# Gated cross-attention block with a Hadamard feed-forward: chunk 0 by halves of the channels, LayerNorm 2 of chunk 0 applied behind gate and up

## The reference

```python
# per channel, over t:  y_t = (A*p + E*v_t) / (A*q + E), in closed form sums of
# exp(k_s + decay*(t-s)) * v_s over the same without v_s
x = x + tanh(g_xattn[0]) * wkv(w, u, k=layernorm(x), v=ctx)
# feed-forward of h = layernorm(x), 256 -> 1024 -> 256
h = fwht(h * SU_ug) / 64
up, gate = h @ W_up.T * (s_up * 64), h @ W_gate.T * (s_gate * 64)
h = fwht(silu(gate) * up * SU_dp) / 64
x = x + tanh(g_ffn[0]) * (h @ W_down.T * (s_dp * 64))
```

## Time and profile before

| | us |
|---|---|
| median of 3 runs | 118.2 (117.4 to 118.34) |
| span of the profiled execution | 117.3 |
| TensorE busy | 99.5 |
| VectorE busy | 70.0 |
| ScalarE busy | 67.6 |
| POOL busy | 61.3 |

### The profile page before, as it was taken

How to read it: one execution, slowest core, us unless ns; L and a number is a source line. 1 busy time by engine, 2 the same in 40 slices (tenths; PEclk the granted TensorE clock), 3 DMA queues, 4 the chain that set the end, 5 groups by cost and what they waited for, 6 DMA issues and landing times.

```text
span 117.3 us, 1942 instructions
## 1 busy us (share of the span) xinstructions
PE 99.5 (85%) x684; PEld 89.2 (76%) x684; DVE 70.0 (60%) x145; ACT 67.6 (58%) x146; POOL 61.3 (52%) x76
## 2 busy tenths in 40 slices
PE   0056584799969999999999999999999999869980
PEld 0044463664559978789999999999999999769970
DVE  0688289936696798797998456874137531231311
ACT  4589566013689942999562899645459732504400
POOL 7102899689909897953550805732520633222430
PEclk9999999999999999999999999999999999999999
DMA  2799999200000000000000020000020000020002
GB/s 72 171 329 409 334 399 408 101 0 3 0 3 6 0 0 0 0 0 6 0 0 0 3 95 0 0 0 0 6 89 0 3 0 6 0 89 0 3 0 89
DMA packets 3074, 7.69 MB, mean 66 GB/s; under 512 B 468, under 2 KB 854, under 8 KB 2936
## 3 DMA queue, kind: packets, MB, share of 16 engines
q1 hardware_dynamic: 3064, 7.57, 17.9%
HBM read 6.52 MB, written 1.05 MB: 65 GB/s over the span
## 4 chain that ended last, share of the span: by engine, by line
PE 70%; DMA 9%; DVE 8%; ACT 4%; SPq 3%; issue 2%; POOL 1%; POOLq 1%; ACTq 0%; DVEq 0%
PE UG L900 38%; PE OD L938 12%; DMA V<-in_ct 9%; PE KZ L938 6%; PE UG L827 5%; PE FX L859 5%; PE FX L868 2%; DVE X L327 1%; DVE XT L762 1%; PE VB L876 1%; DVE SP_ L640 1%; SPq L389 1%; ACT S L596 1%; DVE OD L705 1%; PE VB L881 1%
## 5 line engine op out<-in xcount | busy, mean ns | idle before, releaser
L461 POOL TENSOR_TENSOR HL<-H,HH 128x256 fp32r<-128x256 f32 x32 | 25.7, 813 | 32.4 <-ACT HH L587 32.4
L776 DVE SCALAR_TENSOR_TENSOR H<-S,ALPHA,UG 128x256 f32<-128x256 f32 x32 | 15.0, 478 | 22.3 <-ACT S L596 22.1
L596 ACT ACTIVATE S<-UG,VT 128x256 f32<-128x256 f32 x32 | 15.1, 472 | 17.5 <-PE UG L900 17.4
L900 PE MATMUL UG<-FH,WTH 128*128 128x256 f32 x128 | 21.4, 289 | 0.8 <-ACT FH L581 0.8
L900 PE MATMUL UG<-FL,WTH 128*128 128x256 f32 x128 | 20.4, 281 | 0.0
L900 PE MATMUL UG<-FH,WTL 128*128 128x256 f32 x128 | 20.3, 280 | 0.0
L900 PEld LDWEIGHTS UG<-FH,WTH 128*128 128x128 f32 x128 | 17.8, 189 | 2.1 <-issue 1.9
L900 PEld LDWEIGHTS UG<-FH,WTL 128*128 128x128 f32 x128 | 17.4, 189 | 0.0
L900 PEld LDWEIGHTS UG<-FL,WTH 128*128 128x128 f32 x128 | 17.4, 188 | 0.0
L587 ACT ACTIVATE HH<-H 128x256 fp32r<-128x256 f32 x32 | 13.2, 412 | 4.5 <-DVE H L776 4.2
L938 PE MATMUL OD<-HH,MH 128*128 128x256 f32 x40 | 11.3, 283 | 1.6 <-DVE XT L762 1.6
(11 more groups left out here) (120 smaller groups left out, 200.5 us busy)
## 6 DMA issues: line engine op xcount, KB each, us to landing
WN<-in_weights SPq DMA_DIRECT2D x4, 512.0 KB, 9.8
DN<-in_w_down SPq DMA_DIRECT2D x1, 1024.0 KB, 8.6
out<-XT SPq DMA_DIRECT2D x3, 256.0 KB, 2.5
V<-in_ct SPq DMA_DIRECT2D x2, 258.0 KB, 10.8
V<-in_ct SPq DMA_DIRECT2D x1, 516.0 KB, 12.5
X<-in_x SPq DMA_DIRECT2D x2, 256.0 KB, 4.2
XT<-in_xt SPq DMA_DIRECT2D x2, 256.0 KB, 10.8
X<-in_x SPq DMA_DIRECT2D x1, 512.0 KB, 11.5
```

Source lines behind the costliest of these rows:

```text
L461: pool.tensor_tensor(HL[:, q % JT, 0:n], ring(H, q), HH[:, q % JT, 0:n].bitcast(F32), ALU.subtract).then_inc(h_lo, 1)
L596: act.activation(ring(S, q), gate_part(q), ACT.Silu, scale=VT[:, V_SGATE + j:V_SGATE + j + 1]).then_inc(silu_ready, 1)
L776: dve.scalar_tensor_tensor(out=ring(H, q), in0=ring(S, q), scalar=ALPHA[:, j:j + 1], in1=up_part(q), op0=ALU.mult, op1=ALU.mult).then_inc( ...
L900: return pe.matmul(dst.rearrange("p (g n) -> p g n", n=GT), w[:, m, j, t, :], f[:, chunks, t, :], start=start, stop=stop, skip_group_check ...
```

## The change

- **Chunk 0 by halves.** Its WKV runs as stages with names ending in 0, each on one half of the channels (256 columns), in two PSUM banks of their own. Its values are multiplied with the gate tanh in `av0`; y goes to `YT`, and the transform is made in parts, x (`x_part`) and each half of y (`y_part`). POOL adds y to x later (`x1_0`).
- **LayerNorm 2 of chunk 0 behind gate and up.** The raw transform is split (`raw_hi`, `raw_lo`) and multiplied in slots 0 to 3; VectorE scales both halves of the bank there (`scale`). From slot `RAW` = 4 on the scaled `F0` is used.
- **LayerNorm 2 elsewhere.** The variance lands with tokens on partitions (`var`: one column), POOL takes the power -1/2 (`rstd2`), TensorE spreads it (`spread`), ScalarE copies the row (`row`).
- **The down product of chunk 0 unsplit:** two f32 products a slot, from `H0` and `DB`; no high and low parts in slots 0 to 7. `m_hi` and `m_lo` serve later chunks.
- **A third level of butterflies** (`fly` 8 to 11) on VectorE, and one product for each `m`.
- All weights arrive turned; `w` is one product with the identity. The centred matrix comes from TensorE whole. The ramp is an iota on POOL. Two small loads go to ScalarE's queue, and SP's order is new. `LAG` is 5.

The tables and the queue:

```diff
+RAW = 4
 
 
 PE_STAGES = {
-    -1: [("keys", 0), ("center", 0), ("w", 0), ("w_rest", 0), ("w", 1), ("w", 2), ("w", 3), ("w_rest", 1), ("w_rest", 2), ("w_rest", 3),
-        ("keys", 1), ("fwht", 0), ("m", 0), ("ones", 0), ("keys", 2), ("m", 1), ("m_rest", 0)],
-    0: [("keys", 3), ("m_rest", 1)],
-    4: [("m", 2), ("fwht", 1)],
-    5: [("m_rest", 2), ("ones", 1), ("m", 3)],
-    7: [("m_rest", 3)],
-    11: [("fwht", 2)],
-    12: [("ones", 2)],
-    19: [("fwht", 3)],
-    21: [("ones", 3)],
+    -1: [("keys0", 0), ("keys0", 1), ("center", 0), ("w", 0), ("w", 1), ("w_rest", 0), ("x_part", 0), ("keys", 1), ("w", 2),
+        ("w_rest", 1), ("y_part", 0), ("w_rest", 2), ("y_part", 1), ("w", 3)],
+    0: [("var", 0), ("w_rest", 3)],
+    1: [("spread", 0), ("m", 0)],
+    2: [("m", 1)],
+    3: [("m", 2), ("keys", 2), ("m", 3)],
+    4: [("fwht", 1)],
+    5: [("var", 1)],
+    6: [("spread", 1)],
+    7: [("keys", 3)],
+    10: [("fwht", 2)],
+    11: [("var", 2)],
+    12: [("spread", 2)],
+    17: [("fwht", 3)],
+    20: [("var", 3)],
+    21: [("spread", 3)],
 }
 ACT_STAGES = {
-    -1: [("setup", 0), ("signs", 0), ("decay", 0), ("keys", 0), ("pads", 0), ("w_hi", 0), ("w_lo", 0), ("recip", 0), ("w_hi", 1),
-        ("w_hi", 2), ("w_lo", 1), ("w_hi", 3), ("w_lo", 2), ("w_lo", 3), ("w_hi", 4), ("square", 0), ("keys", 1), ("rstd2", 0),
-        ("m_hi", 0), ("w_hi", 5), ("f_hi", 0), ("m_lo", 0), ("m_hi", 1), ("keys", 2), ("recip", 1), ("m_lo", 1), ("keys", 3)],
-    0: [("w_hi", 6)],
-    3: [("w_hi", 7), ("square", 1), ("m_hi", 2)],
-    5: [("m_lo", 2), ("exp_block", (("rstd2", 1), ("recip", 2))), ("m_hi", 3), ("f_hi", 1)],
-    6: [("m_lo", 3)],
-    9: [("x_hi", 2)],
-    11: [("square", 2)],
-    12: [("exp_block", (("rstd2", 2), ("recip", 3))), ("f_hi", 2)],
-    17: [("x_hi", 3)],
-    19: [("square", 3)],
-    20: [("exp_block", (("rstd2", 3),))],
+    -1: [("setup", 0), ("signs", 0), ("pads", 0), ("keys0", 0), ("keys0", 1), ("decay", 0), ("center", 0), ("w_hi", 0),
+        ("w_hi", 1), ("recip0", 0), ("w_lo", 0), ("recip0", 1), ("w_hi", 2), ("w_hi", 3), ("keys", 1), ("w_lo", 1),
+        ("raw_hi", 0), ("w_lo", 2), ("w_hi", 4), ("square", 0), ("w_hi", 5), ("w_hi", 6), ("recip", 1), ("w_lo", 3),
+        ("w_hi", 7), ("row", 0), ("m_copy", 0), ("silu", 0), ("m_copy", 1), ("m_hi", 0), ("f0_hi", 0), ("m_hi", 1),
+        ("m_copy", 2), ("m_hi", 2)],
+    0: [("exp_block", (("keys", 2),))],
+    1: [("m_copy", 3)],
+    2: [("square", 1)],
+    4: [("m_hi", 3)],
+    5: [("row", 1)],
+    7: [("f_hi", 1), ("exp_block", (("keys", 3), ("recip", 2))), ("x_hi", 2)],
+    8: [("square", 2)],
+    9: [("exp_block", (("recip", 3),)), ("row", 2)],
+    12: [("f_hi", 2)],
+    13: [("x_hi", 3)],
+    16: [("square", 3)],
+    20: [("row", 3)],
     21: [("f_hi", 3)],
 }
 DVE_STAGES = {
-    -1: [("stats1", 0), ("setup_rows", 0), ("norm1", 0), ("setup_shift", 0), ("stats1", 1), ("center", 0), ("scan_a", 0), ("mix_den", 0),
-        ("av", 0), ("scan_av", 0), ("mix_num", 0), ("norm1", 1), ("estimate", 0), ("newton", 0), ("x1", 0), ("stats1", 2), ("stats1", 3),
-        ("outs", 0), ("scan_a", 1), ("mix_den", 1), ("root", 0), ("f_scaled", 0), ("av", 1), ("f_lo", 0), ("scan_av", 1), ("mix_num", 1),
-        ("estimate", 1), ("newton", 1), ("x1", 1)],
-    3: [("scan_av", 2), ("scan_a", 2), ("mix_den", 2)],
-    5: [("scan_a", 3), ("mix_num", 2), ("root", 1), ("f_scaled", 1), ("estimate", 2), ("f_lo", 1)],
-    6: [("newton", 2), ("x1", 2)],
-    8: [("mix_den", 3), ("scan_av", 3), ("mix_num", 3), ("x_lo", 2)],
-    12: [("root", 2), ("f_scaled", 2), ("f_lo", 2)],
-    15: [("estimate", 3)],
-    16: [("newton", 3), ("x1", 3), ("x_lo", 3)],
-    20: [("root", 3), ("f_scaled", 3)],
-    21: [("f_lo", 3)],
+    -1: [("pads0", 0), ("stats1", 0), ("rows", 0), ("norm1", 0), ("shift", 0), ("stats1", 1), ("scan_a0", 0), ("mix_den0", 0),
+        ("scan_a0", 1), ("av0", 0), ("mix_den0", 1), ("scan_av0", 0), ("av0", 1), ("mix_num0", 0), ("scan_av0", 1),
+        ("estimate0", 0), ("mix_num0", 1), ("estimate0", 1), ("newton0", 0), ("newton0", 1), ("scan_a", 1), ("mix_den", 1),
+        ("av", 1), ("raw_lo", 0), ("scan_av", 1), ("var_eps", 0), ("mix_num", 1), ("fly", 8), ("fly", 9), ("estimate", 1),
+        ("stats1", 2), ("fly", 10), ("f_scaled", 0), ("newton", 1), ("norm1", 2), ("fly", 11)],
+    0: [("outs", 0)],
+    1: [("f0_lo", 0), ("x1", 1)],
+    2: [("stats1", 3)],
+    3: [("scan_a", 2), ("var_eps", 1), ("mix_den", 2)],
+    4: [("norm1", 3), ("f_scaled", 1), ("scan_av", 2), ("f_lo", 1)],
+    5: [("mix_num", 2)],
+    6: [("estimate", 2)],
+    7: [("newton", 2), ("x1", 2), ("x_lo", 2)],
+    8: [("scan_a", 3)],
+    9: [("mix_den", 3), ("var_eps", 2), ("scan_av", 3), ("mix_num", 3), ("estimate", 3), ("f_scaled", 2)],
+    11: [("newton", 3), ("x1", 3)],
+    13: [("f_lo", 2)],
+    15: [("x_lo", 3)],
+    17: [("var_eps", 3)],
+    19: [("f_scaled", 3)],
+    20: [("f_lo", 3)],
 }
 POOL_STAGES = {
-    -1: [("rstd1", 0), ("rstd1", 1), ("fly", 0), ("fly", 1), ("fly", 2), ("error", 0), ("fly", 3), ("fly", 4), ("fly", 5), ("fly", 6),
-        ("rstd1", 2), ("rstd1", 3), ("norm1", 2), ("fly", 7), ("w_lo", 4), ("norm1", 3), ("av", 2), ("error", 1), ("av", 3), ("w_lo", 5)],
-    2: [("w_lo", 6), ("sum", 1), ("w_lo", 7)],
-    4: [("error", 2)],
-    9: [("sum", 2)],
-    11: [("error", 3)],
-    18: [("sum", 3)],
+    -1: [("rstd1", 0), ("fly", 0), ("fly", 1), ("rstd1", 1), ("norm1", 1), ("fly", 2), ("error0", 0), ("error0", 1),
+        ("fly", 3), ("fly", 4), ("fly", 6), ("fly", 5), ("fly", 7), ("rstd2", 0), ("w_lo", 4), ("error", 1), ("rstd1", 2),
+        ("w_lo", 5), ("w_lo", 6), ("m_lo", 0), ("m_lo", 1), ("av", 2), ("w_lo", 7), ("sum", 1), ("rstd1", 3), ("m_lo", 2),
+        ("rstd2", 1), ("x1_0", 0), ("error", 2), ("av", 3), ("sum", 2), ("m_lo", 3)],
+    3: [("rstd2", 2)],
+    8: [("error", 3)],
+    16: [("sum", 3)],
+    17: [("rstd2", 3)],
 }
 
 
@@ -115,20 +137,19 @@
 
 
 
...
+            if n >= 8:
+                wait_shared(eng, "fly", 4, 5, 6, 7)
+                s = [DN[:, 4 * i + 2 * (n % 2):4 * i + 2 * (n % 2) + 2, :].rearrange("p j c -> p (j c)") for i in range(2)]
+                eng.tensor_tensor(m_part(DB, n - 8), *s, ALU.subtract if n >= 10 else ALU.add).then_inc(done, 1)
+                return
...
 
             load_x(0)
-            sp.dma_start(VT[:, :], vecs).then_inc(vec_in, 16)
-            sp.dma_start(VR[:, :], rows).then_inc(row_in, 16)
             sp.dma_start(HI[:, :], consts).then_inc(const_in, 16)
-            sp.dma_start(STEP[:, :, :].rearrange("p t n -> p (t n)"), steps).then_inc(step_in, 16)
             load_x(1)
+            sp.dma_start(DN[:, :, :], w_down).then_inc(down_in, 16)
+            load_ctx(0)
             load_w(0, 0)
-            sp.dma_start(DN[:, :, :], w_down).then_inc(down_in, 16)
+            load_xt(0)
             load_w(1, 0)
-            load_ctx(0)
-            load_xt(0)
+            load_ctx(1)
             load_w(0, 1)
             load_w(1, 1)
+            load_xt(1)
             load_x(2)
-            load_ctx(1)
-            load_xt(1)
             load_ctx(2)
             load_xt(2)
             for g in range(LAST):
@@ -416,17 +474,18 @@
 
         @block.gpsimd
```

The new functions and stages (semaphore bookkeeping cut):

```diff
+                elif name == "m_copy":
+
+                    act.wait_ge(m_full, M_FULL.index(g) + 1)
+                    act.activation(m_part(DB, g), fill(("m", g))[:, :], ACT.Copy).then_inc(m_copied, 1)
...
+                elif name == "raw_hi":
+
+                    act.wait_ge(f_full, 1)
+                    for t in range(CT):
+                        act.activation(FH[:, FIRST, t, :], FX[:, t * GT:(t + 1) * GT], ACT.Copy).then_inc(raw_hi, 1)
...
-                act.wait_ge(filled, FILLED["up" if width(q) == GT else "gate", q])
+                if q < RAW:
+                    act.wait_ge(scaled, q + 1)
+                else:
+                    act.wait_ge(filled, FILLED["up" if width(q) == GT else "gate", q])
                 act.activation(ring(S, q), gate_part(q), ACT.Silu, scale=VT[:, V_SGATE + j:V_SGATE + j + 1]).then_inc(silu_ready, 1)
-                if q:
+                if q > JT:
                     hi(q - 1)
 
             for q in range(-1, SLOTS):
...
+            def first(name, t):
+
+                part = slice(t * GB * PAD, (t + 1) * GB * PAD)
+                steps, decay = EXPS0[t][:, 0:GB * PAD], D[:, t, :, :].rearrange("p b q -> p (b q)")
+                if name == "scan_a0":
+                    dve.wait_ge(padded_set, t + 1)
+                    dve.wait_ge(pads0, CT)
+                    dve.wait_ge(pads, 3)
+                    dve.wait_ge(a0_ready, t + 1)
+                    dve.tensor_tensor_scan(SQ[:, part], decay, steps, 0.0, ALU.mult, ALU.add).then_inc(scanned_a0, 1)
+                elif name == "mix_den0":
...
+                elif name == "av0":
+                    if t == 0:
+                        dve.wait_ge(ctx_in[0], 16)
```

(72 more changed lines are left out.)

598 lines of the change are left out of this document (337 added, 261 removed).

## The result

The changed kernel takes 121.5 us (median of 4 runs, 121.2 to 123.4); the kernel before took 118.1 us beside it. The ratio is 1.026, with a 95% interval of 1.020 to 1.032: slower, where 116.4 us and faster were forecast. The profiled execution took 121.39 us with a span of 119.6 us, against 117.3 us of span before.

The account below looks back on a forecast made before the run. Bound: the start of TensorE's unbroken stretch plus its work in it. Span 117.3 - 1.7 - 0.7 - 0.35 + 1.0 = 115.5 us; the same step from the median 118.2 gives 116.4 us, range 113.0 to 119.8.

Parts of the forecast that it names:

- part 1: Start to raw transform of chunk 0: second weight piece at 13.8 us, clock rise at 19.0, transform full at 23.3.
- rival 4: Start not brought forward: second weight piece at 14.8 us or later, or a queue holds the halves; 117.4 to 118.4; chance 0.18.
- Part 2: Raw transform to up(4): VectorE's list before hidden(0) sets up(4) at 38.8 us against 40.5, -1.7 us.
- part 3: TensorE's work from up(4) on: products and rests gone, others added, -0.7 us in sum.
- part 4: The tail: LAG 5 leaves five pairs of down products, one more first half fills a wait, -0.35 us.
- part 5: New stalls, up(4) to up(14): VectorE's 27.9 us of work against TensorE's 26.9, +1.0 us, ends 0 and +5.0.
- Rival 2: VectorE bounds groups 0 and 1, its SBUF passes stretched beside POOL: 122 us, 120 with two thirds; chance 0.17.
- rival 1: VectorE's SBUF instructions take their lower ends: up(4) at 36.8 us, no stall, 113.5 us; chance 0.23.
- rival 3: TensorE's clock rises late: lower level until the raw transform, full at 28.4 us; time 121.5 us; chance 0.07.
- idle TensorE of over 3 us between 40 and 70 us: Sign that the forecast is wrong and Rival 2 holds.
- VectorE over 95% busy: Sign that the forecast is right: VectorE's busy share from 25 to 60 us.

Follow-up runs that it names:

- e3: Kernel before with its two small loads (vectors and decay row) issued by ScalarE: 117.9 us, ratio 1.000.
- e10: Kernel before with the two output instructions of a finished chunk ahead of the hidden product of their slot: 117.0 us, ratio 0.985.
- e16: Changed kernel with a third setting of the engines' lists for slots 7 to 14, nothing computed otherwise: 119.9 us, ratio 1.022 to the kernel before.
- e5: Changed kernel with the reciprocal of chunk 2 ahead of the keys of chunk 3 on ScalarE: 121.5 us, ratio 1.026 to the kernel before.
- e7: Changed kernel with POOL's four low parts of M and its addition for chunk 0 cut to one column: 118.8 us, ratio 1.011 to the kernel before.
- e15: Changed kernel with only the block of chunk 3 loosened (some VectorE and ScalarE steps moved to slots 10 and 11): 121.5 us, no ratio.
- e12: Changed kernel with LAG 4 instead of 5: 123.8 us, ratio 1.034 to the kernel before.
- e9: Changed kernel, VectorE's block of chunk 3 spread over slots 9 to 12, chunk 2's transform, variance and spread one slot later: 124.9 us, ratio 1.050.
- e13: Changed kernel with a second setting of the engines' lists for slots 7 to 17: 123.7 us, ratio 1.048 to the kernel before.
- e14: e13 with the two output instructions of each chunk ahead of the hidden product of their slot: 122.6 us, ratio 1.038 to the kernel before.

## Why the prediction was wrong

**The start, part 1: right.** The second weight piece was there at 14.6 us (4.37 + 10.26), 0.8 later than forecast and 0.2 short of rival 4's mark of 14.8 (its products began at 13.55 before), TensorE's records are fast from 17.8 us (forecast 19.0), the raw transform is full at 23.0 us (forecast 23.3).

**Part 2, up(4) at 38.8 us: nearly right, and worth less than it seemed.** It came at 39.22 us. The four butterflies took 4.9 us instead of 3.4: two at the lower bound of 0.68, two at 1.76, above the upper bound of 1.27 (least, median and most of the four, in ns):

```profile
L419 DVE TENSOR_TENSOR DB<-DN x4: 682/1222/1766, 27.4 to 35.2; 128x512 f32<-128x512 f32 x4
```

The rule of the Trainium skill quoted there (SBUF — State Buffer, Who interferes with whom) is borne out where the two meet: 1.76 us is the 0.68 of the instruction and 1.08 of the 1.27 to 1.3 that POOL's instruction beside it takes alone. It held for two of the four butterflies only. norm2 took 2.10 us, near the 2.02 of the pair in the earlier trace rows. The list ended only 0.5 us late all the same, since the transform was 0.3 us early and the steps beside butterflies and norm2 took about 0.9 us less than priced. The comparison was off as well, since the profiled execution of before was a late one: e3, which differs up to there in two small loads only, had up(4) at 38.42 us, and e10, with the same code up to there, at 40.84, with the clock at its lower level from 22 to 28 us. Twelve profiles of the kernel after and of kernels like it up to slot 4 have it between 37.4 and 40.3 us, 39.1 on average. Against the mean of the three profiles of before, 39.9, the gain of the start is about 0.8 us rather than 1.7 (an estimate, for the three lie 2.4 us apart).

The ledger of the span, by the landmarks, in us:

| | forecast | measured |
|---|---|---|
| part 2, up(4) | -1.7 | -1.1 |
| part 3, TensorE's work from up(4) on | -0.7 | -0.1 |
| part 4, LAG 5 and the tail | -0.35 | -0.3 |
| part 5, new stops | +1.0 | +3.8 |
| sum | -1.8 | +2.3 |

**Part 3 was mis-sized by 0.6 us.** Without the four waits, up(4) to up(14) would take 31.1 - 3.8 = 27.3 us, where I had 26.9; the kernel before took 28.7, and LAG 5 took a pair of down products (0.71) out, so the work fell by 0.7, not by 1.05. From up(14) to the end of the last up product it takes 41.6 us (70.34 to 111.92) instead of 41.0 (69.04 to 110.01): +0.6, where +0.35 was forecast. The rows of the single groups were right (f32 pair 0.86 us, keys 3, spread 0.45, variance 0.34). What was missing lies between groups, in tenths: 0.2 around the transform of chunk 1 (up(4) to up(5) is 1.42 + 1.73 by rows, and takes 3.36), 0.1 behind the first variance. An up product behind the one-column variance takes 1.51 to 1.53 us instead of 1.42. A change between f32 and split products alone costs nothing: in e16 an unsplit pair and the up product behind it take 2.28 us (53.14 to 55.42), 0.86 + 1.42. What takes these tenths is not shown.

**Part 4 was right.** One pair less ahead of the last up (-0.71), and a tail of 7.7 us (111.9 to 119.6) instead of 7.3 (110.0 to 117.3): -0.3. The wait for POOL's last low parts is shorter there, not gone: the chain of waits still ends through one, at 112.86 us.

**Part 5 failed in its mechanism, and by 2.8 us.** It took VectorE's durations (23.8 to 31.9 us, middle 27.9) against TensorE's 26.9 and called the difference the stall. The amount was right: VectorE was busy for 27.0 us. But VectorE idled too, for 4.1 us in that stretch, so it was not the bound. The stops hang on chains across engines: at 60.19 us reciprocal of chunk 2 (behind keys 3 on ScalarE; e5's swap takes 0.7 us out), error on POOL, Newton, x1, high part; at 48.25 the eps step, late behind a scan of 2.28 us beside POOL (gone in e7), and POOL's power; at 66.68 POOL's power of 1.55 us (in e7 the wait is gone); at 70.34 six steps, four of them of chunk 3, that stand on VectorE ahead of hidden(10) (gone in e15, with the same work on its list). A sum over one engine has no term for a step's place in its queue. e16 shows what the place was worth: the same steps, 2.6 us less in that stretch and 1.6 us less in all.

**From span to time.** Of the error of 5.1 us, 4.1 lie in the span (119.6 against 115.5). The other 1.0 is the step from span to time: I took 0.9, the distance from the profiled span to the median of other runs. It is 1.74 to 1.86 us in every run here, so the profiled execution of before, span 117.3, took about 119.1 us (an estimate from that distance) and was 0.9 us slower than the median it was set against.

**The rivals.** Rival 2 had the right size (120 to 122) and half the mechanism. Stretching beside POOL is real and was worth 2.1 us of span (e7; 2.4 from up(0) on), but the point from which the rival decides, 31 us of VectorE work, was never reached. Rivals 1, 3 and 4 did not come. Of the signs, idle TensorE of over 3 us between 40 and 70 us came by the slots (3.8 us) and not quite by the brackets (2.5 us); VectorE over 95% busy did not come: 17.4 of 21 us from 39 to 60.

**What stays open.** What takes the tenths between TensorE's groups; why the change still costs 2% with its lists set right; why e12's run at full clock took 123.2 us; and why a clock falls in one run and not in the next.

## What to carry to other kernels

Before a step is moved, follow it through the queues: whose wait stands in front of it, and who stands behind it on each engine. A sum of durations on the busiest engine says how much work there is, not when it is there; three settings of the same lists took 124.9, 123.7 and 119.9 us. And look for a small stop first: one pair of instructions ahead of a wait instead of behind it brought 1.5%, as much as the whole change was forecast to bring.

## What the runs showed of the hardware

**A stop of TensorE can cost its clock as well.** The granted clock was 0.50 after the stop of 4.48 us (e9), 0.55 from 68 to 70 us after one of 2.95 us (e13), and in e12, e14 and e15 0.50 in stretches between 36 and 42 us after stops of 1.35 and 0.81 us that the kernel after has too, without a fall in its profile. The Trainium skill (TensorE: Matmul & The Clock Gate, Part 1) says that the clock falls back to its lower level after idle time, and that what a kernel sees of the clock varies from run to run. The rows agree on both. The lower clock stayed for some 3 to 7 us. In e15 it moved up(5) by 1.3 us (4.63 us from up(4), 3.36 in the kernel after), but up(7) by only 0.8 (10.4 against 9.6 us), because TensorE then came too late to stop ahead of the first spread. These are the clocks of 2 us stretches in e12 (columns as in the earlier trace rows):

```profile
34.00:36.00 2.00, 1.19 (x6) 0.52 (x4) 2.00 (x3) 0.26 (x1) 2.00 (x2) 0.92 0.00 0
36.00:38.00 2.00, 1.49 (x4) 0.64 (x4) 2.00 (x6) 1.97 (x4) 0.22 (x1) 0.50 0.00 0
38.00:40.00 2.00, 2.00 (x11) 2.00 (x11) 1.18 (x2) 1.97 (x4) 1.49 (x2) 0.50 0.00 0
...
44.00:46.00 2.00, 2.00 (x17) 1.92 (x16) 0.00 (x0) 1.92 (x5) 1.24 (x2) 1.00 0.00 0
```

**VectorE's instructions with inputs in SBUF have more than one price.** A butterfly of 512 columns takes 0.68 us alone and 1.76 beside POOL, a scan of 516 columns 1.22 and 2.28; the rows of before had shown no more than 1.27 for the first. The pair of norms, with one SBUF input each, has them as well: 0.73 us at 47.3 us in e7, 2.11 at 33.5.
